# A sandwich block in split precision: fp16 halves turned by DMA, norms on VectorE, all queues reordered

## What is computed

```python
x = x + layernorm(attention(layernorm(x)))       # scores = (x*w_lhs)(x*w_rhs)^T, softmax over the keys, times x
h = silu(lin(x, w1) * s1) * (lin(x, w2) * s2)    # x here: layernorm(x); 128 -> 512
h = gelu(lin(h, h1) * sh1)                       # 512 -> 512
h = gelu(lin(h, h2) * sh2)                       # 512 -> 512
x = x + layernorm(lin(h, w3) * s3)               # 512 -> 128
```

## Time and profile before

| | us |
|---|---|
| median of 3 runs | 546.88 |
| lowest, highest | 544.03, 550.43 |
| span of the profiled execution | 548.2 |
| TensorE busy, share of the span | 485.0, 88% |
| DVE, ACT, POOL busy | 430.9, 393.2, 283.5 |

### The profile page before, as it was taken

How to read it: one execution, slowest core, us unless ns; L and a number is a source line. 1 busy time by engine, 2 the same in 40 slices (tenths; PEclk the granted TensorE clock), 3 DMA queues, 4 the chain that set the end, 5 groups by cost and what they waited for, 6 DMA issues and landing times.

```text
span 548.2 us, 10143 instructions
## 1 busy us (share of the span) xinstructions
PE 485.0 (88%) x2818; PEld 386.8 (71%) x2818; DVE 430.9 (79%) x1160; ACT 393.2 (72%) x657; POOL 283.5 (52%) x568
## 2 busy tenths in 40 slices
PE   0765999999899989989898998989899998999992
PEld 0544777777777768777786877777777776877781
DVE  2873969889797978879697987969698797878762
ACT  3673777878697777868686786878678686875861
POOL 5364143837555472755547384655638365255332
PEclk9977999999999999999999999999999999999997
DMA  7010010100302020020202011020201102020111
GB/s 269 19 50 13 20 59 1 62 37 0 97 0 96 0 96 0 18 77 0 96 0 96 0 40 56 0 96 0 96 0 57 38 0 77 1 77 2 38 39 38
DMA packets 12549, 24.13 MB, mean 44 GB/s; under 512 B 1520, under 2 KB 1520, under 8 KB 12528
## 3 DMA queue, kind: packets, MB, share of 16 engines
q1 hardware_dynamic: 12528, 23.87, 12.6%
HBM read 11.28 MB, written 4.19 MB: 28 GB/s over the span
## 4 chain that ended last, share of the span: by engine, by line
PE 42%; POOL 30%; issue 14%; DVE 9%; ACT 2%; POOLq 2%; DMA 0%; DVEq 0%; SPq 0%
PE hid_bank L353 13%; PE hid_bank L277 10%; POOL x2n L1100 6%; PE score_bank L277 5%; POOL ln_x_rstd L1083 5%; PE mix_bank L277 5%; PE eT_bank L375 5%; POOL xn L1100 4%; POOL w_raw L1095 3%; POOL ln_y_rstd L1083 3%; POOL ln_x_shift L1088 2%; PE score_bank L282 2%; DVE hA_lo L777 2%; POOL ln_y_var_eps L1079 2%; POOL ln_x_scaled_mean L1085 2%
## 5 line engine op out<-in xcount | busy, mean ns | idle before, releaser
L628 ACT ACTIVATE w_raw<-hid_bank,columns 128x512 f32<-128x512 f32 x128 | 88.7, 693 | 25.6 <-PE hid_bank L353 21.0
L353 PE MATMUL hid_bank<-hA_hi,w_hi 128*128 128x512 f32 x256 | 104.6, 409 | 0.4 <-DVE w_raw L805 0.4
L353 PE MATMUL hid_bank<-hB_hi,w_hi 128*128 128x512 f32 x256 | 104.7, 409 | 0.0
L353 PE MATMUL hid_bank<-hA_lo,w_hi 128*128 128x512 f32 x256 | 101.0, 395 | 0.0
L353 PE MATMUL hid_bank<-hB_lo,w_hi 128*128 128x512 f32 x256 | 100.9, 394 | 0.0
L618 ACT ACTIVATE w_raw<-hid_bank,columns 128x512 f32<-128x512 f32 x64 | 43.6, 684 | 40.2 <-PE hid_bank L277 40.2
L777 DVE TENSOR_TENSOR hC_lo<-w_raw,hC_hi 128x512 fp32r<-128x512 f32 x64 | 45.7, 716 | 22.7 <-ACT hC_hi L629 22.6
L610 ACT CAST eT_hi<-eT_bank 128x512 f16<-128x512 f32 x64 | 37.9, 593 | 33.1 <-PE eT_bank L282 32.6
L1079 POOL TENSOR_SCALAR ln_x_var_eps<-ln_x_mean_var 128x4 f32<-128x4 f32 x32 | 9.5, 297 | 99.3 <-DVE ln_x_mean_var L790 98.0
L277 PE MATMUL hid_bank<-x2T_hi,w_hi 128*128 128x512 f32 x128 | 54.5, 426 | 3.7 <-issue 3.2
L805 DVE SCALAR_TENSOR_TENSOR w_raw<-hid_bank,columns,w_raw 128x512 f32<-128x512 f32 x64 | 47.7, 745 | 11.8 <-ACT w_raw L618 11.8
(11 more groups left out here) (85 smaller groups left out, 1229.3 us busy)
## 6 DMA issues: line engine op xcount, KB each, us to landing
x_in<-x_dram SPq DMA_DIRECT2D x16, 256.0 KB, 2.8
x_res<-x_dram SPq DMA_DIRECT2D x16, 256.0 KB, 2.7
x_all<-x SPq DMA_DIRECT2D x16, 256.0 KB, 2.3
x_tail<-x_all SPq DMA_DIRECT2D x16, 256.0 KB, 2.8
out_dram<-w_raw SPq DMA_DIRECT2D x16, 256.0 KB, 2.0
w_raw<-weights_dram SPq DMA_DIRECT2D x5, 512.0 KB, 5.9
w_raw<-weights_dram SPq DMA_DIRECT2D x1, 256.0 KB, 7.3
columns<-columns_dram SPq DMA_DIRECT2D x1, 9.5 KB, 2.4
```

Source lines behind the costliest of these rows:

```text
L353: mm = nc.tensor.matmul(hid_bank[m][:, :], lhs, rhs, start=(k == 0 and n == 0), stop=(k == K - 1 and n == len(pairs) - 1))
L628: nc.scalar.activation(h_full[:, m, :], hid_bank[m][:, :], ACT.Gelu, scale=scale)
```

## The change

The five queues are written anew; what is computed stays. Part by part:
- **e.** PE's `turn_e`, its PSUM bank and ACT's copy out of it go. POOL rounds the unturned `exps` to fp16 (`high_e`), DVE subtracts (`low_e`, both inputs now in SBUF), both halves lie side by side in `e_split` (128 x 1024 fp16 per row tile, 256 KB), and SP issues one transposing DMA of them into `eT`. That makes four DMAs more per batch, 64 in all.
- **Norms.** `xn`, `x2n`, and the normalised attention and FFN outputs are made on DVE in one pass, (x - mean) * rstd. POOL's chain shrinks to variance + eps and the power. The eps of attention is one DVE operation. The two residual additions are 128x512 `tensor_tensor` on POOL.
- **Halves.** `high_A` moves from DVE to ACT; `low_C` and `low_xn` from DVE to POOL. Of the six parts of the weights DVE rounds three (before: ACT), and POOL subtracts three (before: DVE).
- **Banks.** `xT` and `x2T` are turned into the bank of layer 3 and no longer into the score banks.
- **Order.** All queues are reordered. Layer 1 is now split over the loop's edge: step i (5 to 15) holds the end of layer 1, layer 2 and layer 3 of batch i-4 and the gate and most of layer 1 of batch i-3. A `ramp()` stands before the loop and a longer `finish()` behind it.

The core of the diff (new functions and the new loop bodies; start, ramp and finish left out):

```diff
+            def turn_e(a, j):
+                sp.wait_ge(e_lo_ready, a * T + j + 1)
+                apart(sp)
+                wait_free(sp, pv_done, T, a, j + 1 - T)
+                apart(sp)
+                sp.dma_start_transpose(eT[:, j, :, :, :].rearrange("p h t s -> p (h t) s"),
+                                       e_split[:, j, :, :].rearrange("p h s -> p (h s)")).then_inc(eT_landed[j], 16)
 
...
+            def step(i):
+                now = i
+                back1 = i - 1
+                back2 = i - 2
+                back4 = i - 4
+                load_x(now)
+                turn_e(back2, 1)
+                turn_e(back2, 2)
+                turn_e(back2, 3)
+                load_x_res(back1)
+                load_x1_tail(back4)
+                turn_e(back1, 0)
+                save_x1(back2)
+                store(back4)
...
             def attend(b, j):
                 if j == 0:
                     pe.wait_ge(xn_lo_ready, b + 1)
-                    wait_free(pe, y_ready, 1, b, -2)
-                    wait_free(pe, x1_ready, 1, b, 0)
-                pe.wait_ge(eT_lo_ready, b * T + j + 1)
+                pe.wait_ge(eT_landed[j], b * 16 + 16)
                 pairs = []
                 for t in range(T):
-                    hi, lo = eT_hi[:, j, t, :], eT_lo[:, j, t, :]
+                    hi, lo = eT[:, j, 0, t, :], eT[:, j, 1, t, :]
                     pairs += [(hi, xn_hi[:, t, :]), (hi, xn_lo[:, t, :]), (lo, xn_hi[:, t, :])]
                 matmuls(mix_bank[:, j * P:(j + 1) * P], pairs).then_inc(pv_done, 1)
...
+            def layer1(general, b, m, k):
+                pe.wait_ge(hA_lo_ready, b * K + k + 1)
+                hidden(general, b, m, k, H1, hA_hi, hA_lo, h1_mm)
...
+                def step(i):
+                    back1 = i - 1
+                    back2 = i - 2
+                    back3 = i - 3
+                    back4 = i - 4
+                    layer1(general, back4, 1, 3)
+                    layer1(general, back4, 3, 1)
+                    layer1(general, back4, 2, 3)
+                    pe.wait_ge(yT_ready, back1 - 3)
+                    turn_x(back1)
+                    layer1(general, back4, 3, 2)
+                    layer1(general, back4, 3, 3)
+                    pe.wait_ge(gelu1_done, back4 * K + 1)
+                    layer2(general, back4, 0, 0)
+                    pe.wait_ge(gelu1_done, back4 * K + 2)
+                    layer2(general, back4, 1, 0)
+                    pe.wait_ge(gelu1_done, back4 * K + 3)
+                    layer2(general, back4, 2, 0)
+                    layer2(general, back4, 1, 1)
+                    layer2(general, back4, 0, 1)
+                    layer2(general, back4, 0, 2)
+                    layer2(general, back4, 0, 3)
+                    layer2(general, back4, 1, 2)
+                    pe.wait_ge(gelu1_done, back4 * K + 4)
+                    layer2(general, back4, 3, 0)
+                    layer2(general, back4, 1, 3)
+                    layer2(general, back4, 2, 1)
+                    layer2(general, back4, 2, 2)
+                    layer2(general, back4, 2, 3)
+                    layer2(general, back4, 3, 1)
+                    pe.wait_ge(xT_lo_ready, back3 * 2 + 6)
+                    turn_x2(back3)
+                    layer2(general, back4, 3, 2)
+                    layer2(general, back4, 3, 3)
+                    pe.wait_ge(y_n_ready, back2 - 2)
+                    attend(back2, 0)
+                    scores(back1, 0)
+                    pe.wait_ge(x2T_lo_ready, back4 + 2)
+                    layer3(general, back4, 0)
+                    scores(back1, 1)
+                    attend(back2, 1)
+                    pe.wait_ge(gelu2_done, back3 * K - 2)
+                    gated(general, back3, 0)
+                    pe.wait_ge(gelu2_done, back3 * K)
+                    gated(general, back3, 1)
+                    attend(back2, 2)
+                    attend(back2, 3)
+                    layer3(general, back4, 1)
+                    pe.wait_ge(gated_done, back3 * K + 1)
+                    gated(general, back3, 2)
+                    pe.wait_ge(gated_done, back3 * K + 2)
+                    gated(general, back3, 3)
+                    scores(back1, 2)
+                    layer3(general, back4, 2)
+                    pe.wait_ge(gated_done, back3 * K + 3)
+                    layer1(general, back3, 0, 0)
+                    pe.wait_ge(gated_done, back3 * K + 3)
+                    layer1(general, back3, 1, 0)
+                    pe.wait_ge(gated_done, back3 * K + 4)
+                    layer1(general, back3, 2, 0)
+                    pe.wait_ge(gated_done, back3 * K + 4)
+                    layer1(general, back3, 3, 0)
+                    layer3(general, back4, 3)
+                    scores(back1, 3)
+                    layer1(general, back3, 1, 1)
+                    layer1(general, back3, 1, 2)
+                    layer1(general, back3, 0, 1)
+                    layer1(general, back3, 0, 2)
+                    layer1(general, back3, 0, 3)
+                    layer1(general, back3, 2, 1)
+                    layer1(general, back3, 2, 2)
+                    pe.wait_ge(att_n_ready, back4 + 3)
+                    turn_y(back4)
...
+            def high_A(b, m):
+                if m == 0:
+                    wait_free(act, h1_mm, K, b, 0)
+                act.wait_ge(gated_done, b * K + m + 1)
+                nc.scalar.copy(hA_hi[:, m, :], h_full[:, m, :]).then_inc(hA_hi_ready, 1)
...
+            def step(i):
+                back1 = i - 1
+                back3 = i - 3
+                back4 = i - 4
+                high_xT(back1)
+                high_aT(back1)
+                gelu2(back4, 0)
+                gelu2(back4, 1)
+                gelu2(back4, 2)
+                high_x2T(back3)
+                gelu2(back4, 3)
+                softmax(back1, 0)
+                silu(back3, 0)
+                silu(back3, 1)
+                high_A(back3, 0)
+                high_A(back3, 1)
+                silu(back3, 2)
+                silu(back3, 3)
+                softmax(back1, 1)
+                high_A(back3, 2)
+                high_A(back3, 3)
+                softmax(back1, 2)
+                scale_y(back4)
+                softmax(back1, 3)
+                gelu1(back3, 0)
+                gelu1(back3, 1)
+                gelu1(back3, 2)
+                gelu1(back3, 3)
...
-            def scaled_add(norm, b, src, base, base_ready, out, done):
-
-                dve.wait_ge(base_ready, b + 1)
+            def centred(norm, src, out, done):
                 for t in range(T):
-                    op = nc.vector.scalar_tensor_tensor(out[:, t, :], src[:, t * P:(t + 1) * P], norm.rstd[:, t:t + 1],
-                                                        base[:, t, :], ALU.mult, ALU.add)
+                    op = nc.vector.tensor_scalar(out[:, t, :], src[:, t * P:(t + 1) * P], norm.mean_var[:, t, 0:1],
+                                                 norm.rstd[:, t:t + 1], ALU.subtract, ALU.mult)
                 op.then_inc(done, 1)
...
+            def low_e(b, j):
+                dve.wait_ge(e_hi_ready, b * T + j + 1)
+                nc.vector.tensor_tensor(e_split[:, j, 1, :], exps[:, j, :], e_split[:, j, 0, :], ALU.subtract).then_inc(e_lo_ready, 1)
...
+            def normalize_x(b):
+                dve.wait_ge(ln_x.rstd_ready, b + 1)
+                wait_free(dve, xT_turned, 1, b, 0)
+                wait_free(dve, xn_lo_ready, 1, b, 0)
+                for t in range(T):
+                    op = nc.vector.tensor_scalar(xn[:, t, :], x_in[:, t, :], ln_x.mean_var[:, t, 0:1], ln_x.rstd[:, t:t + 1],
+                                          ALU.subtract, ALU.mult)
+                op.then_inc(xn_ready, 1)
...
+            def step(i):
+                now = i
+                back1 = i - 1
+                back2 = i - 2
+                back3 = i - 3
+                back4 = i - 4
+                low_aT(back1)
+                normalize_x1(back3)
+                low_e(back2, 3)
+                low_x2T(back3)
+                x_statistics(now)
+                aggregate(ln_x, now)
+                row_max(back1, 0)
+                row_max(back1, 1)
+                gated(back3, 0)
+                gated(back3, 1)
+                attention_statistics(back2)
+                low_A(back3, 0)
+                gated(back3, 2)
+                aggregate(ln_att, back2)
+                gated(back3, 3)
+                low_A(back3, 1)
+                low_e(back1, 0)
+                row_max(back1, 2)
+                low_A(back3, 2)
+                row_max(back1, 3)
+                low_A(back3, 3)
+                normalize_x(now)
+                normalize_att(back2)
+                low_e(back1, 1)
+                y_statistics(back4)
+                low_B(back3, 0)
+                aggregate(ln_y, back4)
+                x1_statistics(back2)
```

(89 more changed lines are left out.)

1347 lines of the change are left out of this document (762 added, 585 removed).

## The result

| | before | after |
|---|---|---|
| median of the runs, us | 546.75 (544.03 to 550.43) | 555.46 (552.70 to 559.12, 4 runs) |
| ratio to before | 1 | 1.0195, 95% interval 1.0142 to 1.0248 |
| span of the profiled execution, us | 548.2 | 553.5 |
| loop step, us | 31.67 | 31.56 at full clock; 33.1 in three of ten steps and 32.2 in a fourth, clock 0.95 |

The kernel became 2% slower (1.4 to 2.5% by the interval; the two medians alone give a ratio of 1.016). The forecast was 502, with a range of 488 to 538.

A forecast was written before the change was run, and what follows sets the result against it. PE was taken as the bound, with 2.5 us of waits per step. 548.2 less 37.1 (eleven loop steps), 6.6 (three more stages) and 2.5 (start and end) gave 502 us, own range 489 to 515, full range 488 to 538.

The forecast's parts named there:

- T: Time one 256 KB transposing DMA holds the path: taken near 2 us, lower bound 0.34, free up to 2.7.
- The upper bound of 13: Upper bound in us for one transposing DMA, from 8,192 pieces of 32 bytes at 1.6 ns each.
- The rivals on the transposes: Transposes partly in the open, total 526, chance 0.10; transposes bound the kernel, 603 at 5.5 us each, chance 0.14.
- PE's floor: PE's work per loop step without waits: 29.18 us less 1.76 for four turn groups, 27.4 us.
- The normalising pass out of SBUF: DVE's eight pieces per step, between 0.11 and 0.344 us each, taken as 0.2, together 1.6 us.
- POOL and DVE shut each other out: Rival: 20 DVE operations per step may meet POOL's, DVE loses 5 us, step about 30, total 526; chance 0.10.
- The exponential's table: ACT's loop step gets four table loads of 1.283 us instead of three, adding 1.28 to a 25.4 us busy sum.
- ACT takes over: Rival: ACT, 25.4 us busy plus 4.3 of waits, sets a step of 29.7, total 522; chance 0.08.
- Start: Start and end of the kernel together were given a gain of 2.5 us.
- thin covers: In the new step, inputs ready only 0.3 to 0.7 us before PE needs them; some were expected to fail.
- the forecast's step (28.3): Loop step in us: PE's new floor of 27.4 plus 0.9 of waiting, down from 31.67.
- the 0.9 charged: PE's remaining waiting per loop step in us, less than half of the earlier 2.5.

The follow-up runs named there:

- twice: Changed kernel with every transposing DMA issued twice, first into a scratch tile, and SP waiting for the previous scratch copy to land; 586.0 us, single run.
- exp_pre: `wait_x2n` plus a one-column exponential into a spare tile before the first real one in a loop step, loading the table early; 519.44 us, ratio 0.9526.
- wait_x2n: Changed kernel, with POOL in the loop starting its two low_C of batch i-4 only when DVE's x2n pass is done; 535.56 us, ratio 0.9787.
- exp_only: Changed kernel plus only the one-column exponential that loads the table early, POOL's order untouched; 542.05 us, ratio 0.9922.
- start_dve: `best1` with the low halves of weight parts 3, 4 and 5 moved from POOL back to DVE in the start; 512.7 us, ratio 0.9399.
- best1: `wait_x2n`, the same wait once in the start, `exp_pre`, GELU's table also loaded early, and `tail_dve`, all together; 516.29 us, ratio 0.9474.
- tail_dve: `wait_x2n` with low_C of the last two batches moved from POOL back to DVE behind the loop; 536.28 us, ratio 0.9838.

## Why the prediction was wrong

**Turns and DMA: right.** The loop lost its turn groups, and the transposes never held PE: T was 1.3 to 1.5, between my bound of 0.34 and my value of 2. Landing took 3.4 us, not under 3. The upper bound of 13 rested on a misreading: the trace has the columns' 9.5 KB as 128 packets of 76 bytes, and nearly all the other small packets are of 4 bytes, so 1.6 ns a packet is no price of that transfer. The sum did not use it. The rivals on the transposes fell. `twice` shows how close they were: with a pair of transposes each 3.4 to 3.8 us the kernel is 30 us slower still. In `exp_pre` five weight loads in 160 us already waited for `eT`, 1.9 us in all.

**PE's floor: 27.86 for 27.4.** A small miss, 14 x 0.46 = 6.4 us. A product behind a joint costs about 0.1 more (309.51 to 309.82 is 0.31 for 0.23), but I have not counted the joints, so where the 0.46 lies is open.

**The normalising pass out of SBUF: the step that failed.** Under "DVE" I bounded a piece from above by 0.344, took 0.2, and under "PE after the change" let `normalize_x1` end at 9.0 against the turn at 9.3. A piece took 0.787 on average, and the block at 301.41 took 3.34 us instead of 0.8. The upper bound was not one. Nor was the 0.344 for the passes out of PSUM, which took 0.402. The earlier trace rows had shown that an operation on SBUF takes twice its time beside POOL, and the change puts 0.61 + 2.50 us of POOL's reading beside just this pass. The rival "POOL and DVE shut each other out" had the mechanism. But I spread it as chance over 20 operations, priced it at half a POOL operation each, and concluded "most DVE work is not late". The order of the queues is fixed, so it meets the same instruction in every step. Of DVE's miss (26.6 for 22.6) x2n is 4 x 0.59 = 2.3, `xn` 0.6, `hA_lo` 0.6, the passes out of PSUM 0.5 and the subtractions for e 0.3. The Trainium skill (SBUF — State Buffer, Who interferes with whom) says that such pairs exclude each other fully, and the block of 3.34 beside POOL's 3.1 agrees, in that a piece lasted about as long as the POOL instruction beside it (1.32 and 1.30 for 0.34 alone). What it cost: 2.15 us per step and the clock's 1.5 in four of ten, together 2.7 us a step, of which `wait_x2n` won back 2.0, some 20 us in all; the rest went into the next wait.

**The exponential's table: also failed, silently.** I added a fourth load of 1.28 to ACT's sum, found 25.4 (measured 25.2), and was content with "the queue fits". The prediction has the load as busy time alone, with no place on the path. But the load starts only when the exponential's own wait ends. The loads and SiLU then stand between the row maxima and the gate. `exp_pre` and `exp_only` give 13 to 16 us for it. The rival "ACT takes over" (522) had looked for this in ACT's sum, where it was not: in `exp_pre` ACT is busy 25.5 of 29.00, little more than the 25.2 of the kernel after, and PE no longer waits at the gate. The Trainium skill (ScalarE: Activation LUTs, What ACT_TABLE_LOAD costs) has about 2.66 us per switch, 1283 ns of load and 1380 ns of drain. The trace has the 1.28 alone: the load at 311.01 ends at 312.29, and the next instruction, the one-element SiLU, starts at 312.30.

**Start: I expected a gain, it lost 4.7.** At least the larger part is the same exclusion, which I had not looked for outside the loop: `start_dve` took 4.7 us off the start of `best1` in the profiles, and 3.6 off the median.

**Stage 14: +3.5, open in part.** PE waits for nothing longer than 0.7 in it. It is busy 24.83 us there, 21.98 before, so more of its work lies behind that mark in the new order. `tail_dve` excludes the low halves on POOL. Whether another order of the end would win those microseconds wasn't tried.

**The chances.** I gave 0.58 to thin covers that mostly hold and 0.14 to a slower kernel, by the DMA alone. It became slower by another cause. No rival combined two losses, and the one with the right mechanism was held to 526. With the two losses taken away (`exp_pre`) the forecast's step (28.3) was met within 0.3 us, partly by luck, since the floor was 0.46 too low and the waits left were 28.6 - 27.86 = 0.7 for the 0.9 charged. The total was met within 18 us, and in `start_dve`, with the start and smaller things mended too, within 11.

## What to carry to other kernels

Where two engines shut each other out, as DVE and POOL do on SBUF here, lay their queues side by side and look for the one place where a short operation on the path meets a row of wide ones on the other engine: it will meet it in every iteration, and cost the whole row. Here one wait that orders the two won most of it back. The load of a function table started only behind the wait of the instruction that needed it (308.92, behind 1.20 us of waiting); a one-element call of the same function ahead of the wait hid it.

## What the runs showed of the hardware

- A DVE pass of 128x128 from SBUF to SBUF took 0.34 us alone and up to 1.33 beside one of POOL's wide operations, 0.84 on average in a block of four (3.34 / 4); a 128x512 subtraction 0.68 alone and 2.85 beside one POOL operation of 2.54.
- POOL's `tensor_tensor` of 128x512 took 1.29 (fp32r out), 1.23 (fp16 out), and 1.48 to 1.51 for the additions of f32.
- The clock fell to the 1.2 GHz level behind the 2 us wait in four of ten steps of the kernel after (33.10 for 31.56 us), in three of ten in `exp_only` with the same wait, and in no loop step of before, where the profile has the wait at 1.80 and not at 1.98 to 2.01. What decides it stays open.
- A transposing DMA of 256 KB of fp16 out of SBUF held SP's queue for 1.3 to 1.5 us and landed 3.4 us after its issue. The 64 of them raised the packets under 512 bytes from 1,520 to 69,104, 1,056 each: 1,024 of 256 bytes and 32 of 4 bytes.
